# Moving a quarter of two products by one slot, and one small vector operation by four, in a fused attention and gating kernel

## The chip, the cores and the metric

One core of a Trainium2 chip runs the whole kernel. The metric is the time on the device in microseconds (us), the median of the runs. TensorE is called PE here, VectorE DVE, ScalarE ACT, GpSimd POOL and SyncE, which issues nearly all transfers, SP. PE's matmuls write PSUM, eight banks of 128 partitions by 512 float32.

## The reference: what is computed

`x` is 4 sequences of 2048 tokens by 512. After a layer norm two attentions of 16 heads of 32 run on it, and their outputs are added to `x`:

```python
xn = layernorm(x)
# causal linear attention, feature map elu + 1
q, k, v = phi(xn @ wq), phi(xn @ wk), xn @ wv
o = cumulative(q, k, v) / (q . cumsum(k) + 1e-6)       # per head
# softmax attention, no mask
q2 = (normalised(xn @ Wq.T + bq) + query_embedding) * softplus(temperature)
h = softmax(q2 @ (xn @ Wk.T + bk).T / sqrt(32)) @ (xn @ Wv.T + bv)
gain = f(top-3 of softmax(h @ Wr.T + br), softmax(h @ Ws.T + bs))   # one number per token
out = x + o @ wo + (h * gain) @ Wp.T + bp
```

## The kernel before

**Groups, blocks and steps.** Heads are taken four at a time (one group: 128 columns), so there are 4 sequences x 4 groups = 16 group passes, each in 4 blocks of 512 queries: 64 blocks. A step `s` does the softmax attention of block `s`. Each step also prepares block `n = s + 4` (all six projections, the linear attention), finishes block `mp = s - 1` and brings the output of earlier tokens out. Steps -4 to -1 only prepare. Steps 0 to 15 bring nothing out. Steps 16 to 59 each make one tile of 128 tokens of the output (`out_tile(s) = s - 16`): the o product (`o @ wo`) and the h product (`h @ Wp`). Steps 60 to 63 (`LIGHT` = 60 on) prepare nothing and do the output of the last tiles. Input tiles are normalised and turned until step 43; steps 44 to 59 have none. Every fourth step (14, 18, ... 58) computes the gates of a block, in slot 11.

**Slots.** A step has 16 slots, one for each tile of 128 keys (`kt` is the slot). In each slot PE computes the scores of this tile (`score`, L1238: 12 matmuls in four row tiles, into banks 0 to 3), then weighs the values with the exponentials of the slot before (`weigh`, L1252, 8 records), then does some extra work. ACT takes the exponential of all four score banks at once (L913, `prob`), three buffers deep, and DVE adds it to `acc` (L1795) for the denominator. There is one set of score banks, so `score` of the next slot waits for this slot's exponential:

```python
            def score(m, kt, wide):
                i = m * TT + kt
                pe.wait_ge(exped, 2 * i)
```

Every engine executes its queue in the order in which the code is written. The order of the extra work is an order written out by hand, slot by slot, in the `step` functions of each engine. On PE, from step 16 on:

| slot | extra work of PE |
|---|---|
| 0 | query projection |
| 1 | turn of the linear denominators (L1133), softmax denominators (`total`, L1122) |
| 2 | sums of squares of q, key projection |
| 3 | numerators of the linear attention |
| 4 | values' projection, first half: `project_v(n, 0)`, 96 matmuls, into bank X2 |
| 5 | `sum_k` (L1193, one matmul), `turn_x` (L1061, four transposes, bank X0; until step 43) |
| 6 | values' projection, second half: `project_v(n, 1)`, 96 matmuls, bank X2 |
| 7, 8 | `turn_r` (L1188), linear key projection (X0) |
| 9, 10 | linear query projection (X2); in every fourth step `mean_k` (L1139, X0) |
| 11 | `turn_phk` (L1198, four transposes, X1); in gate steps the gates (L1219, X0) |
| 12 | o product, 48 matmuls (`branch`), bank X2 |
| 13 | `key_values` (L1162), `key_query(n, 0)` (L1153, X0 and X2) |
| 14 | h product, 48 matmuls, bank X1 |
| 15 | `linear_den` (heads_v), `key_query(n, 1)` |

Nearly all products are float16 pairs (high and low part), and are issued by `by_columns` (L1087): each as four matmuls of 32 columns each, which run side by side in four column tiles of the array.

**The values.** ACT copies each half of the values' projection out of X2 (`keep_v`, L850 and L851, semaphore `v_kept`): the first in its slot 4, behind the exponential of slot 4 and ahead of that of slot 5. The second half reuses X2, so it waits for `v_kept` of the first.

**The softmax output.** `keep_out` (ACT, slot 0) copies the output of block `mp` to `hm`, `divide_h` (DVE, slot 8) divides it in place, `split_h` on ACT (slot 9, L903) writes its high part `h_hi`, and `split_h` on DVE (slot 14, L1810) its low part `h_lo`, which reads `hm` and `h_hi`. SP stores both in slot 14 (L502, L507). The gates of a later step and the h product load them again (`load_use`, L518, buffers `fin`).

**The adds.** `add_o` (DVE, slot 13, L1816) adds the o product from X2 to the output row `y`; `key_query(n, 0)` in PE's slot 13 overwrites X0 and X2 and so waits for it (`yo_done`). `add_h` (DVE, slot 15, L1822) adds the h product from X1; `linear_den` in PE's slot 15 waits for that (`y_done`).

**A key mean.** In every fourth step `mean_k` leaves a row in X0 in slot 9, which DVE's `shift_k` (L1594) reads in its slot 10.

## Time and profile before

| | |
|---|---|
| three runs | 3901.83, 3902.53, 3903.34 us, median 3902.53 |
| the profiled execution | 3900.47 us, of which the span of the trace is 3898.6 |
| PE busy | 3707.3 us, 95% of the span |
| DVE busy | 3360.9 us, 86% |
| ACT busy | 2657.4 us, 68% |
| POOL busy | 450.0 us, 12% |
| granted TensorE clock, mean | 0.989 |

Busy time is a sum over stages. PE's is modelled at the ends of matmuls, and since matmuls overlap, the start of one to the start of the next is the surer measure; the views below give starts. A bracket behind an instruction gives the idle time of its engine just before it and what ended it. The trace's span begins with the first instruction and leaves out what lies before and behind it, so the execution's time is a little longer.

### The profile page before, as it was taken

How to read it: one execution, taken by the hardware profiler on the slowest of the kernel's cores; microseconds unless marked ns; L12 is line 12 of the kernel's file. 1: busy time of each engine (PE TensorE's matmuls, PEld its weight loads, DVE VectorE, ACT ScalarE, POOL GpSimd, SP SyncE). 2: the span in 40 equal slices, each digit the busy share in tenths (PEclk: the TensorE clock that was granted, in tenths of full speed). 3: DMA queues.
4: the chain of work that ended last, by engine and by line, in shares of the span. 5: the costliest groups of instructions: out<-in, count | busy, mean ns of one | idle time of the engine just before them, and what ended most of it. 6: DMA issues, size and time to landing. Idle time of an engine off the chain costs nothing.

```text
span 3898.6 us, 147670 instructions
## 1 busy us (share of the span) xinstructions
PE 3707.3 (95%) x65984; PEld 1742.7 (45%) x65984; DVE 3360.9 (86%) x3595; ACT 2657.4 (68%) x2617; POOL 450.0 (12%) x229
## 2 busy tenths in 40 slices
PE   2889999999999999999999999999999999999999
PEld 1544444444444444444444444444444444444333
DVE  5668999999998989888898888889888888888987
ACT  3457777777777677677677676767766766767663
POOL 3101110011001101101100110100110110100121
PEclk8889999999999999999999999999999999999999
DMA  5322212222223323223222322322222222222223
GB/s 208 114 80 61 75 54 62 62 77 59 70 68 91 93 65 96 79 66 93 88 71 80 102 64 85 98 78 79 69 79 63 78 82 61 86 68 58 81 84 113
DMA packets 364209, 315.82 MB, mean 81 GB/s; under 512 B 158168, under 2 KB 312248, under 8 KB 362932
## 3 DMA queue, kind: packets, MB, share of 16 engines
q1 hardware_dynamic: 362852, 297.93, 25.5%
q8 instruction: 523, 8.57, 0.9%
q10 hardware_dynamic: 720, 8.39, 0.5%
q14 instruction: 114, 0.93, 0.1%
HBM read 230.74 MB, written 75.48 MB: 79 GB/s over the span
## 4 chain that ended last, share of the span: by engine, by line
PE 81%; ACT 9%; DVE 4%; issue 3%; SPq 1%; DMA 1%; ACTq 0%; POOL 0%; DVEq 0%; POOLq 0%
PE ps L1087 32%; PE ps L1252 20%; PE ps L1238 19%; ACT prob L913 8%; PE ps L1153 3%; DVE acc L1795 2%; PE ps L1182 2%; PE ps L1122 1%; PE ps L1176 1%; SPq L442 1%; PE ps L1219 0%; PE ps L1162 0%; ACT r L859 0%; DMA xlo_scratch<-xt_lo 0%; DVE xt_lo L1580 0%
## 5 line engine op out<-in xcount | busy, mean ns | idle before, releaser
L913 ACT ACTIVATE prob<-ps 128x2048 f32<-128x2048 f32 x1024 | 1924.1, 1879 | 629.7 <-PE ps L1238 626.6
L1795 DVE TENSOR_TENSOR acc<-acc,prob 128x2048 f32<-128x2048 f32 x896 | 2055.7, 2294 | 88.2 <-ACT prob L913 74.8
L1252 PE MATMUL ps<-prob,v 128*32 128x512 f32 x8192 | 1091.2, 605 | 0.0
L1238 PE MATMUL ps<-q_hi,k_hi 32*128 32x512 f16 x4096 | 420.6, 385 | 75.4 <-ACT prob L913 70.3
L1087 PE MATMUL ps<-x_hi,w_hi 128*32 128x512 f16 x4096 | 432.6, 383 | 0.6 <-DVE xt_lo L1580 0.6
L1087 PE MATMUL ps<-x_lo,w_hi 128*32 128x512 f16 x4096 | 432.4, 382 | 0.0
L1087 PE MATMUL ps<-x_hi,w_lo 128*32 128x512 f16 x4096 | 432.0, 382 | 0.0
L1238 PE MATMUL ps<-q_hi,k_lo 32*128 32x512 f16 x4096 | 410.6, 374 | 1.6 <-issue 1.6
L1238 PE MATMUL ps<-q_lo,k_hi 32*128 32x512 f16 x4096 | 410.3, 375 | 0.3 <-issue 0.3
L1252 PEld LDWEIGHTS ps<-prob,v 128*32 128x32 f32 x8192 | 161.4, 108 | 433.0 <-issue 432.9
L1087 PE MATMUL ps<-wop_hi,fin 128*32 128x512 f16 x4096 | 342.3, 380 | 4.9 <-DMA y<-in_x 3.2
L1087 PE MATMUL ps<-w_hi,x_lo 128*32 128x256 f16 x4096 | 305.7, 273 | 2.3 <-issue 2.3
L1087 PE MATMUL ps<-w_lo,x_hi 128*32 128x256 f16 x4096 | 305.9, 273 | 0.8 <-issue 0.7
L1087 PE MATMUL ps<-w_hi,x_hi 128*32 128x256 f16 x4096 | 305.6, 273 | 1.0 <-issue 1.0
L702 POOL TENSOR_TENSOR rstd<-rstd_in,minus_half 128x1 f32<-128x1 f32 x64 | 67.5, 1055 | 2066.2 <-DVE rstd_in L1570 2065.9
L741 POOL TENSOR_TENSOR rn<-ss,minus_half 128x16 f32<-128x16 f32 x64 | 199.9, 3123 | 862.5 <-ACT ss L823 862.5
L1238 PEld LDWEIGHTS ps<-q_hi,k_hi 32*128 32x128 f16 x4096 | 108.2, 91 | 418.4 <-ACT prob L913 261.5
L716 POOL TENSOR_TENSOR y<-y,bp 128x512 f32<-128x512 f32 x64 | 156.4, 2445 | 472.6 <-DMA y<-in_x 472.5
L1087 PE MATMUL ps<-wop_lo,fin 128*32 128x512 f16 x2048 | 204.5, 380 | 0.0
L1087 PEld LDWEIGHTS ps<-x_hi,w_hi 128*32 128x32 f16 x4096 | 131.2, 97 | 144.6 <-issue 80.1
L1087 PEld LDWEIGHTS ps<-x_lo,w_hi 128*32 128x32 f16 x4096 | 129.7, 98 | 145.3 <-issue 81.7
L1087 PEld LDWEIGHTS ps<-wop_hi,fin 128*32 128x32 f16 x4096 | 119.4, 97 | 137.2 <-issue 47.1
(263 smaller groups left out, 4380.8 us busy)
## 6 DMA issues: line engine op xcount, KB each, us to landing
x_hi<-xhi_scratch SPq DMA_DIRECT2D x64, 512.0 KB, 6.1
x_lo<-xlo_scratch SPq DMA_DIRECT2D x64, 512.0 KB, 7.4
x_in<-in_x SPq DMA_DIRECT2D x64, 256.0 KB, 7.0
rq<-rq_scratch SPq DMA_DIRECT2D x64, 256.0 KB
rdl<-rdl_scratch SPq DMA_DIRECT2D x64, 256.0 KB
y<-in_x SPq DMA_DIRECT2D x64, 256.0 KB, 5.9
out<-y SPq DMA_DIRECT2D x64, 256.0 KB, 5.8
rden<-rden_scratch SPq DMA_DIRECT2D x63, 256.0 KB
```

The costliest lines, as they stand in the source:

```text
L442: sp.dma_start(x_in[t][:], x_d[0, token_rows(t), :]).then_inc(x_first[i], 16)
L702: g_.tensor_tensor(rstd[:, i], rstd_in[:, i], minus_half[:, 0:1], ALU.pow).then_inc(ln_pow, 1)
L716: g_.tensor_tensor(y[i][:], y[i][:], bp[:], ALU.add).then_inc(y_biased, 1)
L741: g_.tensor_tensor(rn[:], ss[:], minus_half[:], ALU.pow).then_inc(rn_done, 1)
L913: s_.activation(prob[i % 3][:], ps[:, 0:HG, :], ACT.Exp, bias=-SHIFT, scale=inv_c[:, g:g + 1] if wide else 1.0 / CQK).then_inc(exped, 2)
L1087: last = t_.matmul(dst[tile, :], lhsT[:, tile], rhs, start=start, stop=stop)
L1122: last = t_.matmul(bk[rows32(h), :], ones_v[:], acc[:, h, :], start=True, stop=True)
L1153: last = t_.matmul(to[h % 2][:, cols128(j)], phkT[rows32(h), cols128(j)], phqT[rows32(h), cols128(j)], start=True, stop=True)
L1182: last = t_.matmul(X1[rows32(h), cols128(j)], st[rows32(h), i % NST, :], phqT[rows32(h), cols128(j)], start=False, stop=True, skip_group_c ...
L1238: last = t_.matmul(bank[h], kk[rows32(h), cols128(kt)], qq[rows32(h), :], start=(kk is kh and qq is qh), stop=(kk is kl and not wide))
L1252: last = t_.matmul(bank[OUT][rows32(h), :], v[m // NB % 2][:, kt, rows32(h)], prob[i % 3][:, h, :], start=(kt == 0), stop=(kt == TT - 1))
L1795: v_.tensor_tensor(acc[:], acc[:], prob[i % 3][:], ALU.add).then_inc(summed, 1)
```

## The change

- The first two of four k slices of the first tile of `project_v(n, 1)` (24 of its 96 matmuls) are issued in slot 5, ahead of `sum_k`, in steps 16 to 59. The rest stays in slot 6. Slot 5 so waits for `v_kept` of the first half.
- The o product goes to bank X0, not X2, in the steps without gates (33 of the 44), with its first k slice (12 of 48 matmuls) in slot 11, behind `turn_phk`, and the other three in slot 12. It waits for `kl_part` (the linear key projection copied out of X0) and, in every fourth step, for a new semaphore `k_shifted` (`shift_k` has read its row). The waits of slot 12 for `ql_part`, for the denominators and for the last `yo_done` are left out. In the gate steps the o product stays whole in slot 12 and in X2.
- `h_lo` is computed by DVE in slot 2 of the next step instead of slot 14 (up to step 60), and stored by SP in its slot 4. For that `hm` has two buffers. `h_hi` is stored in slot 12 instead of 14.
- In the gate steps SP loads what the gates and the o product need in slot 6 instead of slot 0.

```diff
--- before.py
+++ after.py
@@ -306,7 +306,7 @@
...
         acc = sb("acc", [P, HG, QN])
-        hm, rden, rden_c = sb("hm", [P, QN]), sb("rden", [P, QN]), sb("rden_c", [HG * BT, P])
+        hm, rden, rden_c = [sb(f"hm{i}", [P, QN]) for i in range(2)], sb("rden", [P, QN]), sb("rden_c", [HG * BT, P])
         h_hi, h_lo = sb("h_hi", [P, QN], F16), sb("h_lo", [P, QN], F16)
...
@@ -355,6 +355,10 @@
...
+        def o_bank(t):
+
+            return X2 if gate_block(t + NB * NB) is not None else X0
+
...
@@ -379,7 +383,7 @@
...
-        mean_done, crow_ready = sem("mean_done"), sem("crow_ready")
+        mean_done, crow_ready, k_shifted = sem("mean_done"), sem("crow_ready"), sem("k_shifted")
         k_proj, khi_done, klo_done, ksq_done, kmax_mm, kmax_red = (
...
@@ -581,10 +585,7 @@
...
                     if kt == 0:
-                        if f is not None and s < LIGHT:
-                            for use in gate_uses(f):
-                                load_use(*use)
-                        if o is not None:
+                        if o is not None and (f is None or s >= LIGHT):
                             load_use("o", o)
...
@@ -613,6 +614,11 @@
...
                         spread(rden, rden_d, rden_c[:], rden_out, rden_in, mp, hm_done)
+                    if kt == 6 and f is not None and s < LIGHT:
+                        for use in gate_uses(f):
+                            load_use(*use)
+                        if o is not None:
+                            load_use("o", o)
                     if kt == 7:
...
@@ -635,9 +641,12 @@
...
                             load_weights(g, LQ_)
-                    if kt == (14 if s < LIGHT else 12) and mp is not None:
+                    if kt == 12 and mp is not None:
                         store_h_hi(mp)
+                    if kt == 12 and mp is not None and s >= LIGHT:
                         store_h_lo(mp)
+                    if kt == 4 and ended(s - 1) is not None and s <= LIGHT:
+                        store_h_lo(ended(s - 1))
                     if kt == TT - 1 and split_group(s) is not None:
...
@@ -888,8 +897,9 @@
...
                 act.wait_ge(weighted, (m + 1) * TT)
-                act.wait_ge(hlo_done, m)
-                s_.activation(hm[:], bank[OUT], ACT.Copy).then_inc(out_kept, 1)
+                if m > 1:
+                    act.wait_ge(hlo_done, m - 1)
+                s_.activation(hm[m % 2][:], bank[OUT], ACT.Copy).then_inc(out_kept, 1)
...
@@ -899,8 +909,9 @@
...
                 act.wait_ge(hm_done, m + 1)
+                act.wait_ge(hlo_done, m)
                 act.wait_ge(h_stored, m * 32)
-                s_.activation(h_hi[:], hm[:], ACT.Identity, bias=bvs[:, g:g + 1]).then_inc(hhi_done, 1)
+                s_.activation(h_hi[:], hm[m % 2][:], ACT.Identity, bias=bvs[:, g:g + 1]).then_inc(hhi_done, 1)
...
@@ -1102,13 +1113,13 @@
...
-            def project_v(n, i, tiles=range(2)):
-                for j in tiles:
-                    for k in range(KC):
+            def project_v(n, i, parts=((0, range(KC)), (1, range(KC)))):
+                for j, ks in parts:
+                    for k in ks:
                         for w, x, first in pairs(k):
...
                                               w[:, V_::LV_ - V_, k, :], first, k == KC - 1 and w is w_lo)
-                if 1 in tiles:
+                if parts[-1] == (1, range(KC)):
                     last.then_inc(v_proj, 1)
...
@@ -1295,6 +1306,9 @@
...
                         project_v(n, 0)
+                    if kt == 5 and n is not None and s >= NB * NB:
+                        pe.wait_ge(v_kept, 2 * n + 1)
+                        project_v(n, 1, ((0, range(2)),))
                     if kt == 5:
...
@@ -1308,12 +1322,13 @@
...
                         pe.wait_ge(v_kept, 2 * n + 1)
-                        project_v(n, 1, (0,) if lag else (0, 1))
+                        rest = (0, range(KC) if s < NB * NB else range(2, KC))
+                        project_v(n, 1, (rest,) if lag else (rest, (1, range(KC))))
                     if kt == 7 and n is not None:
...
                         if lag:
-                            project_v(n, 1, (1,))
+                            project_v(n, 1, ((1, range(KC)),))
                     if kt == 7 + lag and n is not None:
...
@@ -1347,13 +1362,17 @@
...
                             gates(gate_block(s), X0)
+                    if kt == 11 and out_tile(s) is not None and o_bank(out_tile(s)) is X0:
+                        pe.wait_ge(kl_part, n + 1)
+                        if n % NB == NB - 1 and n < NBLK - 1:
+                            pe.wait_ge(k_shifted, n // NB + 2)
+                        branch(X0, ("o", out_tile(s)), 0, (0,))
                     if kt == 12 and out_tile(s) is not None:
-                        if n is not None:
+                        if o_bank(out_tile(s)) is X0:
+                            branch(X0, ("o", out_tile(s)), 0, (1, 2, 3))
+                        else:
                             pe.wait_ge(ql_part, n + 1)
-                        if mp is not None:
-                            pe.wait_ge(den_kept, mp + 1)
-                        pe.wait_ge(yo_done, out_tile(s))
-                        branch(X2, ("o", out_tile(s)), 0)
+                            branch(X2, ("o", out_tile(s)), 0)
                     if s >= LIGHT:
...
@@ -1591,7 +1610,8 @@
...
                 dve.wait_ge(mean_done, g + 1)
-                link(v_.tensor_tensor(cmean[:], X0[0:1, 0:P], bkr[:, gc], ALU.add))
+                v_.tensor_tensor(cmean[:], X0[0:1, 0:P], bkr[:, gc], ALU.add).then_inc(k_shifted, 1)
+                dve.wait_ge(k_shifted, g + 1)
...
@@ -1801,18 +1821,18 @@
...
                 dve.wait_ge(out_kept, m + 1)
-                v_.tensor_tensor(hm[:], hm[:], rden[:], ALU.mult).then_inc(hm_done, 1)
+                v_.tensor_tensor(hm[m % 2][:], hm[m % 2][:], rden[:], ALU.mult).then_inc(hm_done, 1)
...
                 dve.wait_ge(h_stored, m * 32)
-                v_.scalar_tensor_tensor(h_lo[:], hm[:], bvs[:, g:g + 1], h_hi[:], ALU.add, ALU.subtract).then_inc(hlo_done, 1)
+                v_.scalar_tensor_tensor(h_lo[:], hm[m % 2][:], bvs[:, g:g + 1], h_hi[:], ALU.add, ALU.subtract).then_inc(hlo_done, 1)
...
                 dve.wait_ge(y_biased, t + 1)
-                out, src = y[y_at(t)][:], X2 if t < L0 else (X0, X1)[LATE_AT["o", t] % 2]
+                out, src = y[y_at(t)][:], o_bank(t) if t < L0 else (X0, X1)[LATE_AT["o", t] % 2]
                 v_.scalar_tensor_tensor(out, src, u_o[:, 0:1], out, ALU.mult, ALU.add).then_inc(yo_done, 1)
...
@@ -1928,6 +1948,8 @@
...
                         split_q(deferred(s - 1))
+                    if kt == 2 and ended(s - 1) is not None and s <= LIGHT:
+                        split_h(ended(s - 1))
                     if kt == 3:
...
@@ -1959,7 +1981,7 @@
...
                         scale_q(n)
-                    if kt == (14 if s < LIGHT else 12) and mp is not None:
+                    if kt == 12 and mp is not None and s >= LIGHT:
                         split_h(mp)
...
@@ -1989,7 +2011,8 @@
...
             dve.wait_ge(rden_done, NBLK)
-            v_.tensor_tensor(hm[:], hm[:], rden[:], ALU.mult).then_inc(hm_done, 1)
+            last_h = hm[(NBLK - 1) % 2]
+            v_.tensor_tensor(last_h[:], last_h[:], rden[:], ALU.mult).then_inc(hm_done, 1)
             gate_gains(B * NB - 2)
...
```

## Rows read from the trace of the kernel before

**Rows 1.** The page, part 4: chain that ended last, shares by engine and line.

```profile
PE 81%; ACT 9%; DVE 4%; issue 3%; SPq 1%; DMA 1%; ACTq 0%; POOL 0%; DVEq 0%; POOLq 0%
PE ps L1087 32%; PE ps L1252 20%; PE ps L1238 19%; ACT prob L913 8%; PE ps L1153 3%; DVE acc L1795 2%; PE ps L1182 2%; PE ps L1122 1%; PE ps L1176 1%; SPq L442 1%; PE ps L1219 0%; PE ps L1162 0%; ACT r L859 0%; DMA xlo_scratch<-xt_lo 0%; DVE xt_lo L1580 0%
```

**Rows 2.** Waits of PE, steps 16 to 59: us in total, times, longest.

```profile
PE ps L1238 <- ACT prob L913: 40.1, 79, 1.0
```

**Rows 3.** Timeline of PE, step 32, slots 4 to 6: start, us, instruction.

```profile
2050.50 0.29 PE L1087 MATMUL ps<-w_hi,x_hi 128*32 128x256 f16 x4
...
2053.01 0.29 PE L1087 MATMUL ps<-w_lo,x_hi 128*32 128x256 f16 x4
...
2053.99 1.07 PE L1252 MATMUL ps<-prob,v 128*32 128x512 f32 x8
2054.88 0.38 PE L1193 MATMUL ps<-ksq,headmask_b 128*4 128x512 bf16 x1
2055.19 0.66 PE L1061 MATMUL ps<-ident,x_in 128*128 128x128 f32 x4
2056.14 0.39 PE L1238 MATMUL ps<-q_hi,k_hi 32*128 32x512 f16 x4 [0.29 <-ACT prob L913]
```

**Rows 4.** Timeline of ACT, the same slots.

```profile
2054.20 1.88 ACT L913 ACTIVATE prob<-ps 128x2048 f32<-128x2048 f32 x1 [0.19 <-PE ps L1238]
2055.97 0.59 ACT L789 ACTIVATE xt_hi<-ps 128x512 f16<-128x512 f32 x1
2057.09 1.88 ACT L913 ACTIVATE prob<-ps 128x2048 f32<-128x2048 f32 x1 [0.53 <-PE ps L1238]
```

**Rows 5.** Timeline of ACT and PE, step 45, slot 5.

```profile
2805.87 1.88 ACT L913 ACTIVATE prob<-ps 128x2048 f32<-128x2048 f32 x1 [0.19 <-PE ps L1238]
...
2806.55 0.38 PE L1193 MATMUL ps<-ksq,headmask_b 128*4 128x512 bf16 x1
...
2807.89 0.40 PE L1238 MATMUL ps<-q_hi,k_hi 32*128 32x512 f16 x4 [0.96 <-ACT prob L913]
```

**Rows 6.** Timeline of PE, step 32, ends of slots 11 and 12.

```profile
2075.95 0.40 PE L1238 MATMUL ps<-q_hi,k_hi 32*128 32x512 f16 x4 [0.49 <-ACT prob L913]
...
2079.96 0.40 PE L1087 MATMUL ps<-wop_hi,fin 128*32 128x512 f16 x4
2080.29 0.40 PE L1238 MATMUL ps<-q_hi,k_hi 32*128 32x512 f16 x4
```

**Rows 7.** Timeline of PE, gate step 34, slot 11: transposes, then gates.

```profile
2189.93 0.66 PE L1198 MATMUL ps<-ident,phkT 128*128 128x128 f32 x4
2190.42 0.17 PE L1219 MATMUL ps<-wg_hi,fin 128*128 128x17 f16 x1
```

**Rows 8.** Waits over the whole span: DVE before `k_lo`.

```profile
DVE k_lo L1710 <- ACT k_hi L838: 70.7, 58, 3.1
```

**Rows 9.** Timeline of DVE, step 23, slots 13 to 15.

```profile
1559.12 0.75 DVE L1816 SCALAR_TENSOR_TENSOR y<-ps,u_o,y 128x512 f32<-128x512 f32 x1
...
1565.98 0.75 DVE L1810 SCALAR_TENSOR_TENSOR h_lo<-hm,bvs,h_hi 128x512 f16<-128x512 f32 x1
1566.64 0.75 DVE L1822 SCALAR_TENSOR_TENSOR y<-ps,gain_h,y 128x512 f32<-128x512 f32 x1
```

**Rows 10.** Timeline of PE, step 23, slots 13 and 15.

```profile
1560.25 0.94 PE L1153 MATMUL ps<-phqT,phkT 32*128 32x128 f32 x12
...
1566.33 1.06 PE L1252 MATMUL ps<-prob,v 128*32 128x512 f32 x8
1567.49 0.43 PE L1087 MATMUL ps<-heads_v,zc 128*32 128x4 f32 x32
```

**Rows 11.** Timeline of PE, step 8, slot 1.

```profile
675.59 0.38 PE L1133 MATMUL ps<-ident,dl 128*16 128x128 f32 x2 [0.44 <-DVE dl L1770]
```

**Rows 12.** Timeline of PE, step 32, slot 7: full width, then column tiles.

```profile
2062.15 0.27 PE L1188 MATMUL ps<-ident,rns 128*16 128x128 f32 x1
2062.16 0.39 PE L1087 MATMUL ps<-x_hi,w_hi 128*32 128x512 f16 x3
```

**Rows 13.** Timeline of PE, step 9, slot 4: an irregular hole.

```profile
744.36 0.29 PE L1087 MATMUL ps<-w_hi,x_lo 128*32 128x256 f16 x4 [1.44 <-issue]
```

## The prediction

> **What bounds the kernel now.** The chain that ended last was read first [rows 1]: most of it is PE, the next largest piece is the exponential of L913. So PE decides, except where it waits for ACT. The waits of PE alone, taken over the steps that the change touches (16 to 59), say how much that is: PE stood still 40.1 us for `prob`, in 79 places [rows 2]. In this stretch nearly nothing else stops PE. The reader is to see that there are about 40 us to win in these 44 steps by any better spread of PE's own work, and that no other single thing offers as much.
>
> Where do these 40 us lie? A slot is scores, weighing of the slot before, extra work; the next scores need the exponential of this slot to have read the score banks. The timeline of PE in step 32 shows a short slot [rows 3]: slot 5 has only `sum_k` (L1193) and four transposes (L1061) as extra work, and the scores of slot 6 start at 2056.14 after 0.29 us of idleness. ACT had begun the exponential of slot 5 at 2054.20 and ended it at 2056.08 [rows 4]; the scores came 0.06 later. From step 44 the transposes are gone and the idleness is 0.96 [rows 5]. Slot 11, with only the transposes of L1198, has 0.49 [rows 6]. Slots 4, 6, 12 and 14 are long ones, bound by PE. A piece moved from a long slot into a short one shortens the long one by its whole length and lengthens the short one only by what sticks out beyond the exponential.
>
> **The quarter of the values' projection, slot 6 to slot 5 (44 steps).** It is 24 matmuls, four column tiles at a time, six passes. One pass of this shape takes (2053.01 - 2050.50) / 23 = 0.109 us [rows 3], the quarter 0.655. It may start where `sum_k` starts now, 0.89 after the weighing, at 2054.88. `sum_k` then starts at 2055.53, the transposes 0.31 after it as now (2055.19 - 2054.88), at 2055.84. After the start of four transposes the next work can start 0.49 later [rows 7]; row-tiled scores behind wider work cost about 0.11 more (2080.29 - 2079.96 = 0.33 against a pass of 0.22) [rows 6]. The scores of slot 6 then start at 2056.44, not 2056.14: slot 5 grows by 0.30, slot 6 shrinks by 0.655, gain 0.355. Times 28 steps (16 to 43): **9.9 us**.
>
> In steps 44 to 59 `sum_k` moves from 2806.55 to 2807.20 and the slot could end at about 2807.6, before the exponential: 2805.87 + 1.88 = 2807.75 [rows 5]. So slot 5 stays bound by ACT and the whole 0.655 is won. The scores there start 0.14 after the exponential, where they start 0.06 after it when the idleness is short; I take back that 0.08 too. 16 x 0.735 = **11.8 us**; without it 10.5.
>
> The quarter waits for `v_kept` of the first half. ACT does that copy before the exponential of slot 5 (program order), so before 2054.20 [rows 4], 0.68 ahead of 2054.88: no wait. Behind the quarter stand `sum_k` and the transposes, 0.655 later, and for these wait ACT's copy L789 (0.59 long) and DVE. The copy would begin at about 2056.5 and end at 2057.1; the exponential of slot 6, now 0.95 after its scores' start, would be due at 2057.39. It is hidden by 0.25. DVE's `xt_lo` gets about 0.5 later; it is needed only by slot 7's projection, a whole long slot on.
>
> **The quarter of the o product, slot 12 to slot 11 (33 steps).** Eleven of the 44 steps have gates in slot 11 and keep the old order. In the other 33 PE ended the transposes at 2075.95 - 0.49 = 2075.46 [rows 6]; what follows four transposes can start 0.17 before their modelled end (2189.93 + 0.66 against 2190.42) [rows 7], so the column passes start at 2075.29 and take 3 x 0.218 = 0.655; with 0.11 for the switch the scores start at 2076.06 instead of 2075.95. Slot 11 grows by 0.11, slot 12 shrinks by 0.655: 0.54, times 33 = **17.8 us**. The new wait on `kl_part` is for a slot 8 copy, that on `k_shifted` (10 steps) for a small DVE operation of slot 10; behind them queue the product and the next scores. Both are over by slot 11. The waits on `ql_part` and on the denominators in slot 12 fall away, and nothing is late there now, so zero.
>
> **The low part of h, DVE slot 14 to slot 2 of the next step.** Its cost on DVE stays (0.75). Where it goes, DVE has air: before `k_lo` in slot 3 it waits 70.7 us in 58 steps, 1.2 each [rows 8], and what waits on DVE after slot 2 is due in slots 5 and 7. Where that cover is gone, at most 0.66 is pushed onto slots 3 to 7, which have idleness of their own. What it frees shows in two places. In every fourth step DVE is without a pause from slot 10 to the end. First: in step 23 `h_lo` runs at 1565.98 and pushes the add of the h product to 1566.64 [rows 9], and PE's `linear_den` comes at 1567.49, 1.16 after the weighing instead of 0.89 [rows 10]: 0.27 lost, 11 times, 3.0 us, and it would go. Second: in steps 4, 8, 12 and 16 PE waits 0.44 for DVE's reciprocal, which had `h_lo` ahead of it in its queue [rows 11]: **1.8 us** more.
>
> Against that stands a new wait in the same eleven steps. The add of the o product ends at 1559.12 + 0.75 = 1559.87 [rows 9] and `key_query` starts at 1560.25 [rows 10]; about 0.10 must lie between, as between the other add's end (1566.64 + 0.75) and 1567.49. PE arrives 0.54 earlier, DVE does not, since nothing in its queue before this add was removed. PE waits 0.54 - 0.28 = 0.26, 11 times, 2.9 us, just what the first relief gives back. The two cancel.
>
> The store of `h_lo` leaves SP's slot 14, and the gate loads go from slot 0 to slot 6, five slots ahead of their use. In the eleven gate steps ten loads now stand ahead of the stores of x and o and of the spread of rq, which only the next step needs there. `hm` doubled removes a wait that never ended last. The late steps are the same. All of this: zero.
>
> **Sum.** 9.9 + 11.8 + 17.8 + 1.8 + 3.0 - 2.9 = 41.4 us. The profiled execution took 3900.47 (span 3898.6) and would take 3859; the median of the runs, 2.06 above it, is 3902.53 and becomes **3861 us**.
>
> **A rule of the Trainium skill against it.** The row first: behind the two full-width matmuls of L1188 column-tiled ones start at 2062.16, 0.01 after the first and without a hole [rows 12]. The Trainium skill, TensorEngine Tiling (Array Packing), Key Properties, says that a change of tiling mode drains the array. Slot 11 gets one more such change (full width to columns). By the row it costs nothing; by the rule something in each of 33 steps, which is the second rival.
>
> **The rivals.**
> (1) As summed, 3861. For it: every term is a difference of two starts in a steady trace, and no term leans on a price that it doesn't show.
> (2) The added switch of slot 11 drains the array. Between the 0.11 of the switch to row tiles [rows 6] and the 0.27 that one such matmul takes [rows 12]: 3.6 to 8.9 us less, 3865 to 3870. The row of L1087 behind L1188 [rows 12] speaks against it. The Trainium skill's rule above (TensorEngine Tiling (Array Packing), Key Properties) speaks for it.
> (3) DVE holds PE in slot 13 in all 33 steps, not in eleven: 0.26 x 22 = 5.7 us less, 3867; if all that slot 11 gives is lost, 3879. Against it: in the other 22 steps DVE has neither the bound nor the scaling and splitting of q in this stretch.
> (4) The copy L789 ends after the scores of slot 6 and delays the exponential; the gain of steps 16 to 43 is lost, 3871. Against it: the 0.25 of cover.
> (5) Slower: the early quarter finds `v_kept` missing. If ACT came to that copy only after the exponential of slot 5, PE would stand from 2054.88 to 2056.08 + 0.66 + 0.10 = 2056.84, 1.96 a step, 86 us in 44 steps: 3902.5 - 41.4 + 86 = 3947. It decides from 41.4 / 44 = 0.94 us a step, a copy later than 2055.82. ACT's order speaks against it.
> (6) No change: what is freed comes back as other waits. PE also has irregular holes that nothing releases, the longest 1.44 us [rows 13]. They may fall elsewhere when PE's stream shifts; a few us either way, not 41.
>
> **How the numbers follow.** Chances: (1) 0.65, (2) 0.12, (3) 0.10, (4) 0.07, (5) 0.03, (6) 0.03. The likeliest one's own range is 3855 to 3867, from the holes [rows 13] and the 1.3 us of the disputed 0.08. To hold 8 in 10 it reaches over (2) and most of (3) and (4): 3854 to 3874. Faster by over 0.2% (7.8 us, about what a measurement here can tell from no change): 0.94; within 0.03; slower 0.03.
>
> **What would show it.** In the new trace, slot 6 and slot 12 are 0.65 us shorter; PE's wait for `prob` over steps 16 to 59 falls from 40.1 us to some 7; the scores behind the new slot 5 start 3.2 us after those before it up to step 43, and 2.9 from step 44; `key_query` waits 0.26 in every fourth step and in no other; `linear_den` comes 0.9 after the weighing in all. Wrong would be: a hole between L1198 and the o product, a wait of PE on ACT's `vl` in slot 5, `prob` in slot 6 released by `xt_hi` and not by the scores.

## The result, and the profile after

| | before | after |
|---|---|---|
| median, runs on the same chip | 3902.18 us (3900.78 to 3903.34) | 3872.89 us (3870.57 to 3874.46) |
| ratio, 95% interval | | 0.9922 (0.9910 to 0.9934) |
| profiled execution / its span | 3900.47 / 3898.6 | 3873.82 / 3870.4 |

The kernel is 29.3 us faster by the medians, 26.7 by the two profiled executions. The forecast was 3861, a gain of 41.4, with 3854 to 3874 as the range. So direction and range held. The range held by 1 us, and one of the four executions (3874.46) lies just beyond it. The time lies outside the 3855 to 3867 that was given for the likeliest case alone, and a good quarter of the summed gain is missing. Where it went is the question of this part.

Lines have moved: L913 is now L924, L1087 L1098, L1238 L1249, L1252 L1263, L1193 L1204, L1061 L1072, L1198 L1209, L1153 L1164, L1816 L1836.

The chain that ended last, shares by engine and line, of the kernel after; it answers to [rows 1]:

```profile
PE 84%; ACT 7%; DVE 4%; issue 3%; SPq 1%; DMA 1%; POOL 0%; ACTq 0%; DVEq 0%; POOLq 0%
```

Waits of PE of the kernel after, steps 16 to 59 (us in total, times, longest), to be held against the one row of [rows 2]:

```profile
PE ps L1249 <- ACT prob L924: 5.4, 17, 0.5
PE ps L1098 <- issue: 5.3, 10, 1.1
PE ps L1164 <- DVE y L1836: 1.2, 1, 1.2
PE ps L1204 <- issue: 0.9, 1, 0.9
PE ps L1072 <- issue: 0.8, 1, 0.8
PE ps L1249 <- issue: 0.4, 1, 0.4
```

The wait for `prob` fell from 40.1 to 5.4 us (some 7 were forecast). What was not forecast stands under it: 7.4 us in which PE waits for nothing that the profile shows ("issue"). The same view of before gives 1.7 and 0.8 us of that. Such holes are irregular, like the one of [rows 13]. Counted in the timelines of all 64 steps, from 0.05 us on, they grew from 7.3 to 11.2 us. Of the 7.3, nine pieces of 0.09 us (0.8 in all) are no such holes: they stand at `linear_den` in slot 15 of every fourth step, behind the late add of the h product, and are gone in the kernel after. Without them it is 6.5 against 11.2. (One of the 11.2, 0.5 us in step 48, stands under `prob` in the view: it begins as the usual wait of 0.31.)

**Slot 5, step 32**, timeline of PE in the kernel after (start, us, instruction); it answers to [rows 3]:

```profile
2040.34 0.29 PE L1098 MATMUL ps<-w_hi,x_hi 128*32 128x256 f16 x4
...
2040.99 0.38 PE L1204 MATMUL ps<-ksq,headmask_b 128*4 128x512 bf16 x1
2041.30 0.66 PE L1072 MATMUL ps<-ident,x_in 128*128 128x128 f32 x4
2041.89 0.40 PE L1249 MATMUL ps<-q_hi,k_hi 32*128 32x512 f16 x4
```

And ACT over the same slot, as in [rows 4]:

```profile
2039.09 0.38 ACT L860 ACTIVATE vl<-ps 128x256 f32<-128x256 f32 x1
2039.66 1.88 ACT L924 ACTIVATE prob<-ps 128x2048 f32<-128x2048 f32 x1 [0.19 <-PE ps L1249]
2041.99 0.60 ACT L798 ACTIVATE xt_hi<-ps 128x512 f16<-128x512 f32 x1 [0.46 <-PE ps L1072]
2042.85 1.88 ACT L924 ACTIVATE prob<-ps 128x2048 f32<-128x2048 f32 x1 [0.26 <-PE ps L1249]
```

The quarter starts 0.87 after ACT's copy `vl` of the first half ended and waits for nothing. `sum_k` comes 0.65 later, the transposes 0.31 after it, the scores 0.59 after these. The median slot 5 of steps 16 to 43 is 3.19 us (2.89 before) and slot 6 3.72 (4.37). The copy `xt_hi` ends at 2042.59, 0.26 ahead of the exponential, which waits for the scores and not for it.

**Step 45**, where the transposes are gone, timeline of PE of the kernel after, as in [rows 5]:

```profile
2789.03 0.38 PE L1204 MATMUL ps<-ksq,headmask_b 128*4 128x512 bf16 x1
2789.72 0.40 PE L1249 MATMUL ps<-q_hi,k_hi 32*128 32x512 f16 x4 [0.31 <-ACT prob L924]
```

Idleness is 0.31 instead of 0.96. The exponential of this slot ran from 2787.70 for 1.88, so the scores still come 0.14 after its end, though PE idled so briefly.

**Slots 11 and 12, step 32**, timeline of PE of the kernel after, as in [rows 6]:

```profile
2059.91 0.66 PE L1209 MATMUL ps<-ident,phkT 128*128 128x128 f32 x4
2060.50 0.40 PE L1098 MATMUL ps<-wop_hi,fin 128*32 128x512 f16 x4
...
2060.94 0.39 PE L1098 MATMUL ps<-wop_hi,fin 128*32 128x512 f16 x4
2061.26 0.39 PE L1249 MATMUL ps<-q_hi,k_hi 32*128 32x512 f16 x4
...
2064.96 0.39 PE L1249 MATMUL ps<-q_hi,k_hi 32*128 32x512 f16 x4
```

The column-tiled product begins 0.59 after the first of four transposes; gates, which stay at full width, begin 0.49 after it [rows 7]. So what runs in column tiles starts 0.10 later behind four transposes than what runs at full width. The median slot 11 is 3.10 (3.00 had been forecast: 2.89 + 0.11), slot 12 is 3.70 (4.34 before).

**Step 23, slots 13 and 15.** DVE's add of the o product and PE's `key_query` and `linear_den` in the kernel after. First the timeline of DVE, as in [rows 9]:

```profile
1549.77 0.74 DVE L1836 SCALAR_TENSOR_TENSOR y<-ps,u_o,y 128x512 f32<-128x512 f32 x1
```

And that of PE, as in [rows 10]:

```profile
1550.66 0.94 PE L1164 MATMUL ps<-phqT,phkT 32*128 32x128 f32 x12
...
1556.75 1.06 PE L1263 MATMUL ps<-prob,v 128*32 128x512 f32 x8
1557.63 0.46 PE L1098 MATMUL ps<-heads_v,zc 128*32 128x4 f32 x32
```

`key_query` now follows the add's end by 0.15 (0.38 before): it waits for the add. `linear_den` comes 0.88 after the weighing instead of 1.16. Both came as forecast, the wait in every fourth step alone.

### The profile page after: what moved, and what is told of

It is laid out like the page before. It is cut to its first block, busy times and chain, and to the rows that moved or that the text cites. A ratio compares the mean times of both kernels' runs of the same rounds, so it can differ in the third digit from the quotient of the medians.

```text
span 3870.4 us, 147623 instructions
## 1 busy us (share of the span) xinstructions
PE 3708.2 (96%) x65983; PEld 1742.1 (45%) x65984; DVE 3362.6 (87%) x3595; ACT 2663.1 (69%) x2617; POOL 447.9 (12%) x229
## 4 chain that ended last, share of the span: by engine, by line
PE 84%; ACT 7%; DVE 4%; issue 3%; SPq 1%; DMA 1%; POOL 0%; ACTq 0%; DVEq 0%; POOLq 0%
PE ps L1098 32%; PE ps L1263 22%; PE ps L1249 19%; ACT prob L924 6%; PE ps L1164 4%; PE ps L1193 2%; PE ps L1133 2%; PE ps L1187 1%; DVE acc L1815 1%; PE ps L1209 1%; SPq L446 1%; PE ps L1072 1%; PE ps L1230 0%; ACT r L868 0%; PE ps L1173 0%
## 5 line engine op out<-in xcount | busy, mean ns | idle before, releaser
L924 ACT ACTIVATE prob<-ps 128x2048 f32<-128x2048 f32 x1024 | 1924.4, 1879 | 604.9 <-PE ps L1249 601.9
L1263 PE MATMUL ps<-prob,v 128*32 128x512 f32 x8192 | 1091.0, 605 | 0.0
L1249 PE MATMUL ps<-q_hi,k_hi 32*128 32x512 f16 x4096 | 420.0, 384 | 40.6 <-ACT prob L924 35.2
L1098 PE MATMUL ps<-x_hi,w_hi 128*32 128x512 f16 x4096 | 433.4, 383 | 0.4 <-DVE xt_lo L1599 0.4
L1098 PE MATMUL ps<-x_lo,w_hi 128*32 128x512 f16 x4096 | 433.1, 382 | 0.0
L1098 PE MATMUL ps<-x_hi,w_lo 128*32 128x512 f16 x4096 | 432.9, 382 | 0.0
L1249 PE MATMUL ps<-q_hi,k_lo 32*128 32x512 f16 x4096 | 409.9, 374 | 0.8 <-issue 0.8
L1249 PE MATMUL ps<-q_lo,k_hi 32*128 32x512 f16 x4096 | 409.2, 374 | 0.1
L1263 PEld LDWEIGHTS ps<-prob,v 128*32 128x32 f32 x8192 | 161.1, 108 | 433.2 <-issue 433.2
L1098 PE MATMUL ps<-wop_hi,fin 128*32 128x512 f16 x4096 | 348.8, 381 | 4.3 <-DMA y<-in_x 2.6
L1098 PE MATMUL ps<-w_lo,x_hi 128*32 128x256 f16 x4096 | 306.1, 273 | 3.3 <-issue 3.3
L1098 PE MATMUL ps<-w_hi,x_lo 128*32 128x256 f16 x4096 | 306.0, 273 | 2.9 <-issue 2.7
L1098 PE MATMUL ps<-w_hi,x_hi 128*32 128x256 f16 x4096 | 305.4, 273 | 1.9 <-issue 1.9
L750 POOL TENSOR_TENSOR rn<-ss,minus_half 128x16 f32<-128x16 f32 x64 | 201.7, 3151 | 852.1 <-ACT ss L832 852.1
L1249 PEld LDWEIGHTS ps<-q_hi,k_hi 32*128 32x128 f16 x4096 | 108.0, 91 | 382.8 <-ACT prob L924 236.7
L725 POOL TENSOR_TENSOR y<-y,bp 128x512 f32<-128x512 f32 x64 | 151.9, 2377 | 477.7 <-DMA y<-in_x 477.7
L1098 PE MATMUL ps<-wop_lo,fin 128*32 128x512 f16 x2048 | 204.6, 381 | 0.0
L1098 PEld LDWEIGHTS ps<-x_hi,w_hi 128*32 128x32 f16 x4096 | 131.6, 97 | 143.8 <-issue 80.0
L1098 PEld LDWEIGHTS ps<-x_lo,w_hi 128*32 128x32 f16 x4096 | 130.2, 97 | 145.0 <-issue 81.7
L1098 PEld LDWEIGHTS ps<-wop_hi,fin 128*32 128x32 f16 x4096 | 118.6, 97 | 139.8 <-issue 53.2
```

What stands on the lines that cost most here:

```text
L725: g_.tensor_tensor(y[i][:], y[i][:], bp[:], ALU.add).then_inc(y_biased, 1)
L750: g_.tensor_tensor(rn[:], ss[:], minus_half[:], ALU.pow).then_inc(rn_done, 1)
L924: s_.activation(prob[i % 3][:], ps[:, 0:HG, :], ACT.Exp, bias=-SHIFT, scale=inv_c[:, g:g + 1] if wide else 1.0 / CQK).then_inc(exped, 2)
L1098: last = t_.matmul(dst[tile, :], lhsT[:, tile], rhs, start=start, stop=stop)
L1249: last = t_.matmul(bank[h], kk[rows32(h), cols128(kt)], qq[rows32(h), :], start=(kk is kh and qq is qh), stop=(kk is kl and not wide))
L1263: last = t_.matmul(bank[OUT][rows32(h), :], v[m // NB % 2][:, kt, rows32(h)], prob[i % 3][:, h, :], start=(kt == 0), stop=(kt == TT - 1))
```

## The experiments

Ratios are to the kernel before on the same chip, with a 95% interval.

**The values' quarter alone.** Of the diff only the parts in `project_v` and its calls in slots 5 and 6.

```diff
 if kt == 5 and n is not None and s >= NB * NB:
     pe.wait_ge(v_kept, 2 * n + 1)
     project_v(n, 1, ((0, range(2)),))
```

> The quarter of the values' projection in slot 5 alone; the o product and the low part of h stay as before. If each part pays by the slots it changes: slot 5 3.19 us and slot 6 3.72 in steps 16 to 43, 2.98 and 3.72 in steps 44 to 59, all other slots as before, so 28 x 0.355 + 16 x 0.655 = 20.4 us less than before, some 3882. If the irregular holes of PE grow because PE reaches the same places of its instruction stream earlier within the burst of transfers, they grow here as well (7.3 us before, 11.2 after) and the gain is 15 to 18 us, 3884 to 3887; if they stay at 7, it is another part that makes them grow. If the parts only pay together (the rival that DVE holds the rest), less than 10 us.

Measured: 3885.62 us, ratio 0.9961 (0.9947 to 0.9975), span 3881.6. Slots 5 and 6 together are 8.2 us shorter in steps 16 to 43 and 10.2 in 44 to 59, against 9.9 and 11.8 summed. Holes stayed at 6.9 us. The time missed the expected 3882 by 3.6, and the gain of 16.9 lies where it had been expected only with more holes. The mechanism stands by the slots; of the 11.8, the 0.08 that was taken back for each of 16 steps (1.3 us) does not exist.

**The o quarter alone.** `o_bank`, `k_shifted`, the block in slot 11 and the shorter one in slot 12.

```diff
 if kt == 11 and out_tile(s) is not None and o_bank(out_tile(s)) is X0:
     pe.wait_ge(kl_part, n + 1)
     ...
     branch(X0, ("o", out_tile(s)), 0, (0,))
```

> The quarter of the o product in slot 11 on bank X0 alone. By the slots of the changed kernel: slot 11 3.10 and slot 12 3.70 in the 33 steps without gates, 0.44 less each, 14.5 us. In every fourth step PE arrives 0.44 earlier at the wait for the add of the o product, which left 0.28: 0.16 to 0.2 lost in slot 13, and with the low part of h still in DVE's slot 14 the wait for the add of the h product stays or grows from 0.26: 11 x 0.2 to 11 x 0.4 lost, gain 10 to 12.5 us, 3890 to 3892. If the wait of slot 13 did not need the low part of h, gain 14.5, 3888. Holes of PE as before, near 7 us, since slots 4 and 5 are untouched.

Measured: 3896.93, ratio 0.9986 (0.9977 to 0.9996), span 3891.8. Slots 11 and 12 gave 14.5 us, not 17.8: slot 11 is 3.10. In every fourth step slot 14 grows from 4.47 to 4.65, as in the kernel after: the wait for `add_o`. Without the later `h_lo` slot 15 grows too (2.89 to 3.07), and PE idles 0.3 before `linear_den`. The time missed what was expected (3890 to 3892) by 5 us. Steps 16 to 59 are 9.2 us shorter. But the first score comes 0.7 later, the part behind the last score is 2.4 longer, and the time outside the span is 3.5 instead of 1.9. This last is no chance: it is 3.1 to 4.2 us in every execution of every kernel with the o quarter, and 1.8 to 2.1 in every execution of the kernel before and of the variants without it. So the o quarter costs some 2 us outside the span; which of its parts does, no run shows.

**h_lo alone.** The two `hm` buffers, DVE's slot 2, SP's slots 4 and 12.

```diff
+if kt == 2 and ended(s - 1) is not None and s <= LIGHT:
+    split_h(ended(s - 1))
-if kt == (14 if s < LIGHT else 12) and mp is not None:
+if kt == 12 and mp is not None and s >= LIGHT:
```

> The low part of h in the next step alone, with the two buffers of hm and the later gate loads. PE's waits in slot 15 of every fourth step (11 x 0.26) and in slot 1 of steps 4, 8, 12, 16 (4 x 0.47) go, nothing else: 4.7 us less, 3897.5. If this part were free of effect, 3902; if SP's freer queue or the gate loads in slot 6 are what makes the holes of PE grow, they grow here from 7 to 11 and the time is 3901.

Measured: 3899.45, ratio 0.9992 (0.9982 to 1.0001), span 3895.2, 3.4 shorter. In steps 20, 24, ... the scores of slot 1 come 4.45 after those of slot 0 instead of 4.71, and PE's wait for the reciprocal in steps 4, 8, 12 and 16 is gone. The two reliefs are there, at about their price (2.7 of the 3.0, and 1.8). By the time alone, 3 us where 4.7 were expected and a ratio of 1 inside the interval, they can't be told from nothing.

**The o quarter ahead of the transposes.** In slot 11 column tiles then follow column tiles (the weighing), and the added change of tiling is gone.

```diff
+if kt == 11 and out_tile(s) is not None and o_bank(out_tile(s)) is X0:
+    ...
+    branch(X0, ("o", out_tile(s)), 0, (0,))
 if kt == 11 + lag:
     ... # turn_phk
```

> The changed kernel with the quarter of the o product ahead of the four transposes of slot 11 instead of behind them. If the 0.10 us that slot 11 got longer than summed is the change of the array from full width to column tiles, it goes away (column tiles then follow the weighing, which uses column tiles too): slot 11 3.00 us in 33 steps, 3.3 us less than the changed kernel, 3869.6. If it is another cost of the quarter (its operands, its bank), slot 11 stays at 3.10 and the time at 3873.

Measured: 3873.13, ratio 0.9920 (0.9904 to 0.9937), span 3870.6. Timeline of PE, step 32, slots 11 and 12, of this kernel:

```profile
2061.66 0.40 PE L1098 MATMUL ps<-wop_hi,fin 128*32 128x512 f16 x4
...
2062.10 0.40 PE L1098 MATMUL ps<-wop_hi,fin 128*32 128x512 f16 x4
2062.43 0.66 PE L1209 MATMUL ps<-ident,phkT 128*128 128x128 f32 x4
2063.01 0.39 PE L1249 MATMUL ps<-q_hi,k_hi 32*128 32x512 f16 x4
```

From the first of these rows to the scores it is 1.35 us, as from the transposes to the scores in the kernel after (2059.91 to 2061.26): both orders change the tiling twice inside this stretch. The change that is saved lies ahead of it, between the weighing and this stretch (0.99 from the weighing to the transposes in the kernel after, 0.88 from the weighing to the first product here). So look at the whole slot: its median is 2.99 instead of 3.10, and it is 0.11 shorter in each of the 33 steps, 3.7 us. That is the price of one change, measured a second way, with the same operands and the same bank. The time doesn't show it (3869.6 had been expected): slot 13 of every fourth step grew by 0.11, since PE came earlier to a DVE that didn't, step 59 alone lost 1.8 in slots 13 and 14, and the holes came out otherwise.

**The holes: the next block's load moved from SP's slot 3 to slot 9.** The load is 1 MB, issued just before PE's slots 4 and 5, where nearly all holes lie.

```diff
 if kt == 3:
     ...
-    if n is not None and n + 1 < NBLK:
-        load_block(n + 1)
+if kt == 9 and n is not None and n + 1 < NBLK:
+    load_block(n + 1)
```

> The changed kernel with both loads of the next x block (1 MB) issued by SP in slot 9 instead of slot 3. Theory: the irregular holes of PE in slots 4 and 5 (21 of the 22, 11.2 us in the changed kernel) come when PE needs the next part of its instruction stream while the x loads and their neighbours fill the transfer engines. Then the holes leave slots 4 and 5 and turn up behind slot 9, in slots 9 to 12, in other steps. If they stay in slots 4 and 5, they have another cause: the rest of the burst of slot 3, or a place in the code. Time: 3873 if they only move, down to 3865 if they fall where PE has air.

Measured: 3862.80 (3859.90 to 3864.53), ratio 0.9895 (0.9878 to 0.9911), span 3860.7. Holes fell from 11.2 us to 3.9, and every slot without a hole kept its length. The slots with holes became 10.2 us shorter in all, more than their idle time says. None came up behind slot 9, where they had been expected, and the time fell below the expected 3865. Why the load does no harm in slot 9 no run shows, nor what makes the 3.9 that stay in slots 4 and 5. Waits of PE in steps 16 to 59 of this kernel:

```profile
PE ps L1249 <- ACT prob L924: 5.5, 17, 0.6
PE ps L1098 <- issue: 2.8, 6, 0.7
PE ps L1164 <- DVE y L1836: 1.2, 1, 1.2
```

Why the load makes PE pause shows in step 33, slot 5. Timeline of PE, kernel after:

```profile
2097.76 0.38 PE L1204 MATMUL ps<-ksq,headmask_b 128*4 128x512 bf16 x1
2098.07 0.33 PE L1072 MATMUL ps<-ident,x_in 128*128 128x128 f32 x1
2099.22 0.38 PE L1072 MATMUL ps<-ident,x_in 128*128 128x128 f32 x2 [0.82 <-issue]
```

The transfers of the kernel after by queue (packets, MB, share of the engines), in the 5.7 us from the start of slot 4, 2091.10 to 2096.80:

```profile
DMA packets 1317, 1.56 MB, mean 273 GB/s; under 512 B 56, under 2 KB 1065, under 8 KB 1316
q1 hardware_dynamic: 1316, 1.55, 92.2%
```

And in the next 1.1 us:

```profile
DMA packets 393, 0.41 MB, mean 375 GB/s; under 512 B 111, under 2 KB 307, under 8 KB 392
q1 hardware_dynamic: 392, 0.40, 102.3%
q8 instruction: 1, 0.02, 5.3%
```

The q8 queue brings instructions, 16 KB a packet. No packet of it came in the first stretch, in which the data queue took 92% of the engines. It came in the second: by its record it started 5.8 us after the start of slot 4 and landed at 2097.82, and PE resumed at 2099.22, 1.4 later. With the load elsewhere the same step looks like this, from the start of slot 4 (2085.95 to 2089.60):

```profile
DMA packets 652, 0.91 MB, mean 250 GB/s; under 512 B 114, under 2 KB 316, under 8 KB 652
q1 hardware_dynamic: 652, 0.91, 79.5%
```

And in its next 1.15 us:

```profile
q1 hardware_dynamic: 407, 0.20, 59.0%
q8 instruction: 1, 0.02, 5.9%
```

Here the packet comes 3.7 us after the start of slot 4, 2.1 earlier, and slots 4 and 5 have no hole. In five steps with long holes (28, 33, 34, 40, 42) the packet was 1.1 to 2.1 later with the load ahead of it. All 14 holes of over 0.3 us in the kernel after end 1.3 to 1.7 us after such a packet has landed. Their places fit: in neighbouring steps they lie 1010 to 1015 matmuls apart in PE's stream, and where both kernels have one in the same step, it stands at the same matmul to within a few. The page of the Trainium skill on this (Runtime: NRT & Kernel Launch, Instruction fetch mechanics) says that PE's buffer is refilled in blocks of 16 KB while the engine runs, at a cost "mostly hidden". The traces agree on the size of a block. Hidden it is here when no large load is ahead of it in the kernel before (0.4 us left, below), and not quite in the kernel after (3.9).

**Half of the load moved** (`x_hi` stays in slot 3, `x_lo` goes to slot 9).

```diff
 if kt == 3:
     ...
-    load_block(n + 1)
+    load_block(n + 1, (0,))
+if kt == 9 and n is not None and n + 1 < NBLK:
+    load_block(n + 1, (1,))
```

> The changed kernel with the high half of the next x block loaded in slot 3 as before and the low half in slot 9. If a hole is PE waiting for its instructions behind a burst of transfers, a burst of half the length makes fewer and shorter holes in slots 4 and 5: under 6 us instead of 11.2, and few new ones behind slot 9; 3866 to 3870. If any transfer of this size delays them as much, 11 us again, spread over both places, 3873.

Measured: 3867.94, ratio 0.9909 (0.9892 to 0.9926), span 3865.1; holes 7.5 us, where under 6 had been expected. Half the load, half the effect.

**The same move in the kernel before.**

> The kernel before with only the load of the next block's inputs (1 MB) issued in SP's slot 9 instead of slot 3. If the irregular holes of PE come from that burst meeting the fetch of PE's instructions whatever the kernel, the 7.3 us of holes of the kernel before fall to under 4, and the time from about 3902.5 to 3897 to 3899. Rival: the holes belong to the changed kernel's longer slot 5, and the holes of the kernel before stay at 7 us and its time within 1.5 us. In either case the slots without holes keep their length.

Measured: 3894.92 (3892.44 to 3896.82, 11 runs), ratio 0.9979 (0.9970 to 0.9988), span 3890.8. Holes fell from 7.3 to 1.2 us, of which 0.9 are the pieces at `linear_den`; so those of the fetch fell from 6.5 to 0.4. Its waits of PE over steps 16 to 59:

```profile
PE ps L1238 <- ACT prob L913: 41.2, 80, 1.1
PE ps L1133 <- DVE dl L1770: 0.4, 1, 0.4
PE ps L1087 <- issue: 0.2, 1, 0.2
```

So the load's price isn't the change's doing, but there are more holes in the changed kernel. What makes them more stays open: each of the three parts alone left those of the fetch (without the pieces at `linear_den`) at 6.1 to 7.2 us. With the load out of the way on both sides the change is worth 3894.92 - 3862.80 = 32.1 us by medians (of two chips), 30.1 by the spans, against 29.3 and 28.2 with it.

**A third slice of the values from step 44 on**, where slot 5 still idles 0.31.

```diff
-project_v(n, 1, ((0, range(2)),))
+project_v(n, 1, ((0, range(2 if t is not None else 3)),))
```

> The changed kernel with three k slices instead of two (36 of 96 matmuls) in slot 5 from step 44 on, where the changed kernel still leaves PE idle 0.31 us before the scores of slot 6. By the same sum that fits the other terms: PE's work of slot 5 then ends 0.33 later, about when the exponential does; slot 5 2.9 to 3.0, slot 6 3.72 - 0.33 = 3.39, so 0.3 to 0.4 less in each of 16 steps, 5 to 6 us, 3867 to 3868. If the 2.98 us of slot 5 is a bound of its own that PE's idleness doesn't set, slot 5 grows by what is put in and nothing is won, 3873.

Measured: 3867.78, ratio 0.9914 (0.9897 to 0.9930), span 3861.4. Slot 6 fell by 0.33 in each of 16 steps, as expected; slots 5 and 6 together gave 4.3 us, with the holes in them.

**`weigh_z` behind `add_o` on DVE.** It runs 0.69 and stood ahead of the add in slot 12.

```diff
-if kt == 12 + lag and n is not None:
+if kt == 12 + lag and n is not None and out_tile(s) is None:
     weigh_z(n)
 ...
     add_o(out_tile(s))
+    weigh_z(n)
```

> The changed kernel with DVE's product of the key sum and phi(q) (L1768, 0.61 us) behind the add of the o product instead of ahead of it. If the 0.2 us that slots 13 and 14 got longer in every fourth step are PE waiting for that add, with DVE never idle before it, they go: slot 14 4.47 instead of 4.65 and slot 13 2.90 instead of 2.93 in all eleven steps, 2.2 us less, 3870.7. If PE waits there for something else, 4.65 stays. linear_den, which needs the moved product, comes two slots later and doesn't wait.

Measured: 3872.92, ratio 0.9921 (0.9904 to 0.9937), span 3869.0. Slots 13 and 14 of every fourth step are back at 2.90 and 4.47, and step 59's wait fell from 1.2 to 0.4; about 3 us in the slots. The time doesn't show it (3870.7 had been expected): 1 us more of holes and 2 us more ahead of the first score stand against it.

**All four together**: the late load, the third slice, `weigh_z` behind the add, the o quarter ahead of the transposes.

> The changed kernel with four edits together: the block's load in SP's slot 9, three k slices of the quarter instead of two in slot 5 from step 44, weigh_z behind add_o on DVE, and the o quarter ahead of turn_phk in slot 11. If they are independent, their slots add up: from 3862.8 (the load alone) 16 x 0.3 = 5 less, 11 x 0.17 = 2 less, 33 x 0.11 = 3.6 less minus 1.2 for the later add_o in every fourth step: about 3853. Rival: DVE holds PE in slot 13 of every fourth step and what slot 11 gives is lost there, and the holes in slots 4 and 5 return with the shifted stream: 3858 to 3862.

Measured: 3851.22 (3849.24 to 3852.57), ratio 0.9866 (0.9851 to 0.9881), span 3848.5. Waits of PE, steps 16 to 59:

```profile
PE ps L1098 <- issue: 1.5, 6, 0.3
PE ps L1164 <- DVE y L1836: 0.5, 1, 0.5
PE ps L1249 <- ACT prob L924: 0.3, 1, 0.3
PE ps L1249 <- issue: 0.2, 1, 0.2
```

Slot by slot the parts add up, and the wait of slot 13 that had eaten part of the o quarter's gain is gone with `weigh_z`. Of the 40.1 us of [rows 2] 0.3 are left. (The view leaves out waits under 0.15 us; with all from 0.02 us on it is 3.1 against 42.9.)

## Why the prediction was right, and what it missed

What was forecast to happen did: PE's waits moved as summed, DVE holds PE in slot 13 of every fourth step and in no other, and neither ACT's `vl` nor its copy `xt_hi` delays anything, so the rivals (3), (4) and (5) did not come. That the time lies inside the range is in part luck. The range was made wide for rivals of which only the second came true, at its lower end; what filled it besides were holes, the end of the kernel and the time outside the span, for which "a few us" had been allowed.

**Values, steps 16 to 43** (9.9 summed). Right: slot 5 came out at 3.19 and slot 6 0.66 shorter, in one step after the other. By the sums of both slots it gave 6.0 here and 8.2 alone, since the holes fall into the same slots; between the two kernels with the late load, where few are left, it gave 9.5.

**Values, steps 44 to 59** (11.8). The mechanism was right, the disputed 0.08 was not: the scores come 0.14 after the exponential here whether PE idles 0.96 or 0.31, so 10.5. Off by 1.3.

**The o product** (17.8). The step that failed is "it costs nothing", the added change from full width to column tiles. Behind four transposes it costs 0.10 (0.59 against 0.49) by the trace, and one change less in the slot gave 0.11. 33 x 0.10 = 3.3 to 3.7 us. That is the second rival at the lower end of its price, and it holds beside the first case, not in place of it. The nothing was read from [rows 12], and that reading was wrong: the matmul of L1188 is no full-width one. Its row says 128*16, so it fills 16 columns, where a transpose says 128*128. The rest of that view of the kernel before shows how the records interleave:

```profile
2062.26 0.27 PE L1188 MATMUL ps<-ident,rns 128*16 128x128 f32 x1
2062.37 0.38 PE L1087 MATMUL ps<-x_hi,w_hi 128*32 128x512 f16 x1
```

Three of the four column products start at 2062.16, beside L1188; the fourth starts at 2062.37, behind its second record. That is what one finds if L1188 sits in one column tile while the other three run: [rows 12] then holds no change from full width to column tiles, and says nothing of its price. The rule of the Trainium skill (TensorEngine Tiling (Array Packing), Key Properties) that was weighed against the row agrees with the 0.10.

**h_lo** (3.0 + 1.8 - 2.9). Right in each part. The slot 0 that follows every fourth step is 0.26 shorter, the reciprocal's wait is gone, `key_query` waits. The last was sized 0.26; slots 13 and 14 grew by 0.03 and 0.18. Beside it step 59 waited 1.2 us, which the prediction had not counted. Timeline of DVE in the kernel after, slots 11 to 13 of that step:

```profile
3610.83 1.78 DVE L1755 SCALAR_TENSOR_TENSOR phqT<-e,r 128x512 f32<-128x512 f32 x1
...
3615.45 0.74 DVE L1836 SCALAR_TENSOR_TENSOR y<-ps,u_o,y 128x512 f32<-128x512 f32 x1
```

And of POOL, the same stretch:

```profile
3610.23 1.83 POOL L725 TENSOR_TENSOR y<-y,bp 128x512 f32<-128x512 f32 x1 [21.11 <-DMA y<-in_x]
```

This DVE operation takes 0.68 in the other steps. Here a POOL operation on the same memory ran beside it, and the add behind it came late. That the one slowed the other is read from the overlap, not tried. It is not any overlap that does it. In step 61 `h_lo` took 1.77 beside the same POOL operation (L725), instead of 0.75. But 48 times `h_lo` lay wholly beside POOL's `rn` (L750, 128x16, 2.9 us) and kept its 0.75.

**The holes.** They were named in the sixth rival and given "a few us either way". They took 4.7 more than before (6.5 to 11.2, without the nine pieces at `linear_den`, which the 3.0 of the h_lo term already holds). What a hole is was left open there, and is shown now; why the change made them more is still open.

**Behind the last score** the kernel after takes 53.9 us, the kernel before 51.5. Granted clock of PE in stretches of this end (columns: busy time of PE, PEld, DVE, ACT, POOL, then the clock, the DMA share and GB/s), of the kernel before:

```profile
3857.00:3862.00 5.00, 5.00 (x72) 2.21 (x68) 1.79 (x2) 0.00 (x0) 3.42 (x4) 0.83 0.99 345
```

And of the kernel after:

```profile
3826.00:3832.00 6.00, 6.00 (x57) 2.44 (x61) 0.64 (x1) 0.00 (x0) 3.13 (x3) 0.57 0.93 312
```

In both PE had stood for a load of `y` (3.15 us before, 2.59 after). The granted clock fell to the lower of its two levels, 1.2 GHz, while PE still stood, and stayed there for 3.4 us before and 6.8 after; of this PE worked 2.8 and 5.2 us. Which of the two a kernel gets followed no part of the change: it was 6.8 too with the load late in the kernel before, 3.4 with the values' quarter or `h_lo` alone. By these figures 2.4 us more at half the clock cost an estimated 1.2 us, half of the difference at the end. Of the rest, waits for a load of `fin` (1.1 us, 0.1 before) less the shorter wait for `y` give 0.4; what remains isn't assigned.

**The sum again**, against the 26.7 of the two profiled executions: 41.4 - 3.3 (tiling) - 1.3 (the 0.08) - 4.7 (holes counted) - 1.2 (step 59) - 2.4 (the end) - 1.5 (the time outside the span, 1.9 before, 3.4 after) = 27.0. That it comes so near is finer than the counts are: the holes cost more than the idle time counted, and the terms of steps 16 to 43 and of `h_lo` are off by some tenths. By medians the gain is 29.3; of the two profiled executions the one before lies 1.7 below its median, the one after 0.9 above.

## What to carry to other kernels

When an engine is bound by its own stream with idle slots between long ones, the start-to-start times of a steady trace price a moved piece to 0.01 us. The seams are what such a sum gets wrong: a change from full width to column tiles cost 0.10, and the pair of rows from which it had been read as free was no such change. Look at the shapes in the rows before you take a price from them. Look at small unexplained holes before the next edit. Here they sat at a fixed distance in the instruction stream with a megabyte of loads in flight, and moving the load by a few slots, one moved statement, was worth 8 to 10 us, about a third of what the whole change gave. And compare the time outside the span as well: here one part of the change lost 2 us there.

## What the runs showed of the hardware that had not been expected

- PE's instructions come by the same transfer engines as the data. In five steps a 16 KB packet came 1.1 to 2.1 us later behind 1 MB of loads, and PE paused by up to 1.1 us (1.4 in the kernel before). In all, PE idled 6.5 us so in the kernel before and 11.2 in the kernel after, and 0.4 and 3.9 with the load elsewhere.
- Full width to column tiles behind four transposes: 0.10 us by the trace. With one change of tiling less, the same slot was 0.11 us shorter in 33 steps.
- A DVE operation of 0.68 us took 1.78 while a POOL operation of 1.83 us ran, and one of 0.75 took 1.77 beside another of the same line; beside the POOL operation on 128x16 elements it kept its 0.75.
- Around a wait of PE of 2.6 to 3.2 us near the end, the granted clock stood at 1.2 GHz for 3.4 us in some kernels and 6.8 in others.
